# Placing the first expert tiles with float32r products of high and low parts, on one Trainium2 core

## The chip, the cores and the metric

The kernel runs on one core of a Trainium2 chip. The metric is the device time of one execution, in microseconds (us). Engines are named as the profile names them: PE is TensorE, DVE is VectorE, ACT is ScalarE, POOL is GpSimd, SP is the engine that issues most transfers.

## What is computed

The reference is a two layer network on x of 4 x 128 rows of 512 numbers. Each layer is a cross attention, a mixer, and a mixture of eight experts of which every row uses two:

```python
x = x + _L0_xattn_ref(...)   # cross attention on 2048 context rows
x = x + _L0_attn_ref(...)    # retention
x = x + _L0_ffn_ref(_layernorm(x, axis=-1), ...)
x = x + _L1_xattn_ref(...)
x = x + _L1_attn_ref(...)    # a linear recurrence
x = x + _L1_ffn_ref(_layernorm(x, axis=-1), ...)

# L0_ffn: two of 8 experts a row, 512 -> 2048 -> 512
logits = silu(x @ rw1 + rb1) @ rw2 + rb2
k_logits, k_index = top_k(logits, 2)
k_prob = softmax(k_logits)
h = silu(xf @ w1[e] + b1[e]) @ w2[e] + b2[e]     # added with weight we of that row and expert
# L1_ffn: two of 8 experts a row, 512 -> 512 -> 512
router_logits = x_flat @ router_w + router_b
activated = silu(sorted_tokens @ we_gate[e]) * (sorted_tokens @ we_up[e])
ff_out = activated @ we_down[e]
```

## The kernel before, in words

The program is six stages in a row, each with its own streams of instructions on the five engines and a barrier between stages. The change is in one function, `stage_experts`, which is run twice: as the third stage (names `moe0_...`, some 836 to 1290 us in the trace, called the first experts here, `first` is true) and as the sixth (`moe1_...`, 2017 to 2210 us, the second experts).

**Precision.** Products that must be exact to float32 are made in one of two ways. A product of two float32 operands is one instruction in the program and two records in the trace. Or both operands are cut into a float32r high part and the float32r rest (hi and lo), and three products are summed in PSUM (`three_products`, lines 91 to 95). Weights are cut this way: ACT casts the block (`high`, L1835), DVE subtracts (`low`, L2012). `lo_done` says that the low part is there.

**Tiles.** The rows that an expert gets are sorted into tiles of 128 slots, 15 tiles (NT). `g` counts groups of 512 hidden columns: 60 groups in the first experts (4 a tile), 15 in the second. For every group PE does `expand` (12 products with 512 columns, `three_products` over four parts of a tile's rows), `turn_h` (4 transposes) and `contract` (12 products). ACT copies the result of `expand` out of PSUM (`kept`, L1926), applies silu (L1937), and casts the next weights. DVE cuts low parts. The tile's own turned rows have to be cut too: ACT casts the bank XB to `xThi` (`high_x`, L1843), then DVE subtracts that from the bank to `xTlo` (`low_x`, L2104), and `expand` waits for it.

**Start of the stage.** Rows are normalised on DVE (`xn`, L1991), turned by PE, the router's scores are made (L1669, L1688), and a chain of small DVE instructions (L2027 to L2064) works out each row's two slots. Then three things go on together:
- POOL scatters the rows `xn` by slot to DRAM with eight indirect transfers (L1631). SP waits for them (`scattered`) and reads the tiles back (`load_rows`, L1579); all later weight loads stand behind this in SP's queue.
- The first tile does not wait for that. DVE writes a matrix of zeros and ones (`here`, L2071, L2074), and PE multiplies `xn` by it (`place_first`, 16 float32 products with 128 columns, L1702) into XB. In the second experts the second tile is made in the same way (`place_next`, L1711).
- The last two tiles (LATE) are never read back row by row: ACT makes their matrices (`late_distances` L1900, `late_shares` L1908), DVE adds them (`add_late`, L2121), and PE turns them (`turn_late`, L1725).

The order on every engine is the order in which the Python code emits it. In the first experts PE has `place_first`, `turn_late` twice, then the groups; ACT has `late_distances`, `late_shares`, `high_x(0)`; DVE has `add_late`, `low_x(0)`, `low(1, 0)`.

Of the kernel before, what the change touches and what calls it, by code (L numbers as in the profile page):

```python
# [25 lines left out]
P = 128  # L26
D = 512
C = D // P
NB = 4
# [1395 lines left out]
def stage_experts(nc, k, name, t, x, x_out, xg, od, layer, prefetch):  # L1425
# [29 lines left out]

    with ExitStack() as ctx:
# [33 lines left out]
        else:  # L1490
# [5 lines left out]
        here = xT[:, 3, :].rearrange("p (b t) -> p b t", b=NB)  # L1496
        next_1st, next_2nd = rows_in[:, 6, :], rows_in[:, 7, :]
        here_next = xT[:, 1, :].rearrange("p (b t) -> p b t", b=NB)
# [24 lines left out]
                                    "we", "we_turned", "weT", "y_made", "y_added", "b1_more", "out", "stored", "summed", "squared", "low_slots", "apart", "near", "next", "late_apart", "low_prob", "late_near")}  # L1523
# [17 lines left out]
        with nc.Block() as block:  # L1541
# [71 lines left out]
            def _(pool):  # L1613
# [14 lines left out]
                nc.gpsimd.tensor_copy(rw2_wide[:, :, 0:NE], rw2[:]).then_inc(s_["wide"], 1)  # L1628
                pool.wait_ge(s_["slots"], 1)
# [12 lines left out]
            def _(pe):  # L1642
# [54 lines left out]

                def place_first():
                    for b in range(NB):
                        pe.wait_ge(s_["here"], b + 1)  # L1700
                        for c in range(C):
                            last = pe.matmul(XB[:, c * P:(c + 1) * P], xn[:, b, c * P:(c + 1) * P], here[:, b, :],  # L1702
                                             start=(b == 0 and c == 0), stop=(b == NB - 1), skip_group_check=True)
                    last.then_inc(x_turned, 1)

                def place_next():
                    pe.wait_ge(xlo_done, 1)
                    pe.wait_ge(s_["next"], 1)
                    for b in range(NB):
                        for c in range(C):  # L1710
                            last = pe.matmul(XB[:, c * P:(c + 1) * P], xn[:, b, c * P:(c + 1) * P], here_next[:, b, :],  # L1711
                                             start=(b == 0 and c == 0), stop=(b == NB - 1), skip_group_check=True)
# [40 lines left out]
                def expand(bank, kind, g):  # L1753
                    i = g // GR
                    pe.wait_ge(lo_done[kind], g + 1)
                    pe.wait_ge(xlo_done, i + 1)
# [764 lines left out]
```

## Time and profile before

| | us |
|---|---|
| median of three runs | 2216.48 |
| lowest and highest | 2208.49, 2216.7 |
| the profiled execution | 2211.86 |
| its span | 2209.9 |
| PE busy in the span | 2097.7 (95%) |
| DVE, ACT, POOL busy | 1395.0, 1390.7, 297.0 |

The profiled execution is one of its own beside the three runs; every duration below is from it. Its span is 2.0 us shorter than its time, which is what lies around the span. In the page's 40 slices the second experts lie in the last three and a half.

### The profile page before, as it was taken

How to read it: one execution, taken by the hardware profiler on the slowest of the kernel's cores; microseconds unless marked ns; L12 is line 12 of the kernel's file. 1: busy time of each engine (PE TensorE's matmuls, PEld its weight loads, DVE VectorE, ACT ScalarE, POOL GpSimd, SP SyncE). 2: the span in 40 equal slices, each digit the busy share in tenths (PEclk: the TensorE clock that was granted, in tenths of full speed). 3: DMA queues.
4: the chain of work that ended last, by engine and by line, in shares of the span. 5: the costliest groups of instructions: out<-in, count | busy, mean ns of one | idle time of the engine just before them, and what ended most of it. 6: DMA issues, size and time to landing. Idle time of an engine off the chain costs nothing. (4 is left out here: it accounts for less than half of the span.)

```text
span 2209.9 us, 37941 instructions
## 1 busy us (share of the span) xinstructions
PE 2097.7 (95%) x14773; PEld 1629.5 (74%) x14773; DVE 1395.0 (63%) x2384; ACT 1390.7 (63%) x2685; POOL 297.0 (13%) x268
## 2 busy tenths in 40 slices
PE   7999999999999989799999989999999999977998
PEld 4788788777775556688888857887877777755775
DVE  6555455455555753699999965445454555577887
ACT  4666566566655444788888845665665666555774
POOL 1212112112100000100000201211111121102001
PEclk9999999999999989999999999999999999998999
DMA  4001000010104002799999830001010010013996
GB/s 162 20 20 40 20 23 37 20 39 20 39 20 149 26 13 99 294 383 381 351 364 363 334 110 20 20 20 39 20 39 20 20 40 20 20 58 115 367 358 236
DMA packets 53792, 262.04 MB, mean 119 GB/s; under 512 B 9576, under 2 KB 9960, under 8 KB 26992
## 3 DMA queue, kind: packets, MB, share of 16 engines
q1 hardware_dynamic: 47312, 244.42, 29.7%
q0 software_dynamic: 2560, 8.39, 1.1%
q10 hardware_dynamic: 3744, 6.82, 0.8%
q8 instruction: 119, 1.95, 0.4%
q14 instruction: 57, 0.47, 0.1%
HBM read 243.61 MB, written 15.99 MB: 117 GB/s over the span
## 5 line engine op out<-in xcount | busy, mean ns | idle before, releaser
L611 DVE COPY c_pt<-bank 128x512 f32<-128x512 f32 x256 | 177.1, 692 | 556.3 <-PE bank L426 556.3
L808 ACT ACTIVATE c_pr<-wide,c_nmax 128x512 f32<-128x512 f32 x512 | 348.9, 697 | 138.7 <-DVE c_nmax L603 71.6
L295 POOL TENSOR_TENSOR c_clo<-land,c_chi 128x512 fp32r<-128x512 f32 x120 | 154.4, 1288 | 992.6 <-ACT c_chi L777 992.6
L426 PE MATMUL bank<-ident,c_pr 128*128 128x128 f32 x2048 | 268.2, 274 | 3.4 <-DVE c_pt L611 2.7
L426 PEld LDWEIGHTS bank<-ident,c_pr 128*128 128x128 f32 x2048 | 239.8, 141 | 37.7 <-DVE c_pt L611 3.6
L791 ACT ACTIVATE c_khi<-bank,c_cols 128x512 fp32r<-128x512 f32 x128 | 88.0, 688 | 252.1 <-PE bank L95 252.1
L93 PE MATMUL bank<-c_wv_hi,c_chi 128*128 128x512 f32 x512 | 218.4, 427 | 18.4 <-DVE c_clo L542 17.1
L93 PE MATMUL bank<-c_chi,c_wk_hi 128*128 128x512 f32 x512 | 214.1, 418 | 0.3 <-DVE c_wk_lo L534 0.2
L94 PE MATMUL bank<-c_wv_lo,c_chi 128*128 128x512 f32 x512 | 203.2, 397 | 0.0
L95 PE MATMUL bank<-c_wv_hi,c_clo 128*128 128x512 f32 x512 | 202.9, 396 | 0.0
L95 PE MATMUL bank<-c_chi,c_wk_lo 128*128 128x512 f32 x512 | 202.5, 395 | 0.0
L94 PE MATMUL bank<-c_clo,c_wk_hi 128*128 128x512 f32 x512 | 199.4, 389 | 0.0
L815 ACT COPY c_pt<-bank 128x512 f32<-128x512 f32 x256 | 150.3, 587 | 63.1 <-PE bank L426 63.0
L603 DVE CUSTOM_DVE_ANT_0 wide<-wide,land 128x512 f32<-128x512 f32 x256 | 169.2, 724 | 3.7 <-PE wide L410 3.3
L606 DVE TENSOR_REDUCE c_nmax<-wide 128x1 f32<-128x512 f32 x256 | 158.9, 684 | 3.4 <-PE wide L410 3.1
L2012 DVE TENSOR_TENSOR moe_wlo<-moe_hr,moe_whi 128x2048 fp32r<-128x2048 f32 x68 | 153.3, 2285 | 5.1 <-ACT moe_whi L1835 5.1
L93 PE MATMUL wide<-moe_whi,moe_xThi 128*128 128x512 f32 x360 | 143.9, 400 | 10.2 <-DVE moe_xTlo L2104 8.4
L93 PEld LDWEIGHTS bank<-c_wv_hi,c_chi 128*128 128x128 f32 x512 | 97.1, 190 | 62.1 <-issue 24.2
L95 PE MATMUL wide<-moe_whi,moe_xTlo 128*128 128x512 f32 x360 | 141.8, 394 | 0.0
L94 PE MATMUL wide<-moe_wlo,moe_xThi 128*128 128x512 f32 x360 | 141.8, 394 | 0.0
L442 PEld LDWEIGHTS bank<-c_pt,c_v 128*32 128x32 f32 x4096 | 104.1, 110 | 48.9 <-issue 46.9
L442 PE MATMUL bank<-c_pt,c_v 128*32 128x128 f32 x4096 | 138.3, 276 | 1.6 <-ACT c_pt L815 1.6
(428 smaller groups left out, 4248.6 us busy)
## 6 DMA issues: line engine op xcount, KB each, us to landing
moe_hr<-in_L_ffn_w SPq DMA_DIRECT2D x68, 1024.0 KB, 7.0
land<-in_L_ffn_w SPq DMA_DIRECT2D x34, 1024.0 KB, 7.6
land<-in_ctx SPq DMA_DIRECT2D x31, 1024.0 KB, 4.9
moe_raw<-in_L_ffn_w SPq DMA_DIRECT2D x18, 1024.0 KB, 7.2
moe_raw<-in_L_ffn_we_gate SPq DMA_DIRECT2D x8, 1024.0 KB, 7.2
land<-in_L_ffn_we_up SPq DMA_DIRECT2D x8, 1024.0 KB, 6.9
moe_raw<-in_L_ffn_we_down SPq DMA_DIRECT2D x8, 1024.0 KB, 8.1
moe_raw<-in_L_ffn_we_up SPq DMA_DIRECT2D x7, 1024.0 KB, 7.7
```

The lines of the kernel that those rows point to most:

```text
L93: pe.matmul(out, w_hi, m_hi, start=start, stop=False, skip_group_check=not check)
L94: pe.matmul(out, w_hi, m_lo, start=False, stop=False, skip_group_check=not check)
L95: return pe.matmul(out, w_lo, m_hi, start=False, stop=stop, skip_group_check=not check)
L295: nc.gpsimd.tensor_tensor(clo[:, g % 2, c, :], raw[:, c, :], f32(chi[:, g % 2, c, :]), ALU.subtract) \
L426: last = pe.transpose(TB[n % 2][:, h * P:(h + 1) * P], pr[:, u % 2, h, n * P:(n + 1) * P], k["ident"][:])
L442: last = pe.matmul(OB[h * HD:(h + 1) * HD, 0:P], v[:, (T4 * g + n) % VR, at:at + HD], pt[:, n, h * P:(h + 1) * P], start=(n == 0), stop=(n ...
L603: nc.vector.tensor_tensor_reduce(S[h][:], S[h][:], hidden[:, i * CH:(i + 1) * CH], -1.0, BIG, ALU.add, ALU.min, into).then_inc(max_done, 1)
L606: nc.vector.tensor_reduce(into, S[h][:], AX.X, ALU.max, negate=True).then_inc(max_done, 1)
L611: nc.vector.tensor_copy(pt[:, n, :], TB[0][:]).then_inc(pt_dve, 1)
L808: nc.scalar.activation(pr[:, u % 2, h, :], S[h][:], ACT.Exp, bias=nmax[:, b % 2, i, at:at + 1], scale=-1.0 if masked else 1.0, accum_out=d ...
L815: nc.scalar.copy(pt[:, n, :], TB[1][:]).then_inc(pt_act, 1)
L2012: nc.vector.tensor_tensor(wlo[kind][:, g % 2, :], raw[n % RW], f32(whi[kind][:, g % 2, :]), ALU.subtract).then_inc(lo_done[kind], 1)
```

## The change

`here`, `here_next` and the rows that are placed become float32r. ACT casts `xn` to `xn_hi` (`high_rows`, four casts of 128x512), POOL subtracts to `xn_lo` (four subtractions of 128x512). `place` multiplies the high parts into XB and the low parts into a second bank, XLO: 32 products where there were 16. Since a matrix of zeros and ones only picks rows, XB then holds the high parts and XLO the low ones, and `low_x` of these tiles is a copy of XLO that waits for PE alone, not for `high_x`. In the second experts ACT takes two of the four copies of the turned rows. In the first experts `high_x(0)` goes ahead of `late_shares`, `low_x(0)` ahead of `add_late`, and `turn_late` behind the first `expand`.

```diff
-        here = xT[:, 3, :].rearrange("p (b t) -> p b t", b=NB)
+        here = hlo[:, 0, :].rearrange("p (b t) -> p b t", b=NB)
+        xn_hi, xn_lo = (tile[KINDS - 1][:, 1, :].rearrange("p (b d) -> p b d", b=NB) for tile in (whi, wlo))
+        XLO = (ps_of[4], ps_of[5])
...
+                if first:
+                    pool.wait_ge(s_["h_made"], HT)
+                for b in range(NB):
+                    pool.wait_ge(s_["xn_hi"], b + 1)
+                    nc.gpsimd.tensor_tensor(xn_lo[:, b, :], xn[:, b, :], f32(xn_hi[:, b, :]), ALU.subtract).then_inc(s_["xn_lo"], 1)
                 pool.wait_ge(s_["slots"], 1)
...
-                        if not first:
+                        if not first and q < 2:
                             pe.wait_ge(s_["xT"], q + 1)
+                        elif not first:
+                            pe.wait_ge(s_["xT_late"], q - 1)
...
+                def place(i, taker, b):
+                    for to, rows in ((XB, xn_hi), (XLO[i], xn_lo)):
+                        for c in range(C):
+                            last = pe.matmul(to[:, c * P:(c + 1) * P], rows[:, b, c * P:(c + 1) * P], taker[:, b, :],
+                                             start=(b == 0 and c == 0), stop=(b == NB - 1), skip_group_check=True)
+                    return last
...
                 place_first()
                 if first:
-                    for l in range(LATE):
-                        turn_late(l)
                     for g in range(NG + 2):
                         if g < NG:
                             after(pe, kept, g - 1)
                             expand(HB[g % 2], 0, g).then_inc(hid_made, 1)
+                        if g == 0:
+                            for l in range(LATE):
+                                turn_late(l)
...
+                def high_rows():
+                    for b in range(NB):
+                        act.wait_ge(s_["xn"], b + 1)
+                        nc.scalar.copy(xn_hi[:, b, :], xn[:, b, :]).then_inc(s_["xn_hi"], 1)
...
+                    high_rows()
                     high(1, 0)
                 else:
+                    high_rows()
+                    for c in (2, 3):
+                        act.wait_ge(s_["turned"], c + 1)
+                        nc.scalar.copy(xT[:, c, :], ps[c][:]).then_inc(s_["xT_late"], 1)
                     high(0, 0)
...
                 if first:
                     late_distances()
+                    high_x(0)
                     late_shares()
-                    high_x(0)
...
                 def low_x(i):
-                    dve.wait_ge(xhi_done, i + 1)
-                    last = nc.vector.tensor_tensor(xTlo[:, i % 2, :], XB[:], f32(xThi[:, i % 2, :]), ALU.subtract)
+                    if i < (1 if first else 2):
+                        dve.wait_ge(x_turned, i + 1)
+                        last = nc.vector.tensor_copy(xTlo[:, i % 2, :], XLO[i][:])
+                    else:
+                        dve.wait_ge(xhi_done, i + 1)
+                        last = nc.vector.tensor_tensor(xTlo[:, i % 2, :], XB[:], f32(xThi[:, i % 2, :]), ALU.subtract)
...
                 if first:
                     weigh_pairs()
+                    low_x(0)
                     add_late()
-                    low_x(0)
                     low(1, 0)
```

How instructions stand on the engines. ACT in the first experts, from the last Silu of the router to the first copy of a hidden group; `moe_e` is the Exp of the router, `moe_in_late` `late_distances`, `moe_prob` `late_shares`, `moe_xThi` `high_x(0)`, the last row `kept(0)`. Before:

```order
L1874 ACTIVATE moe_hr<-bank,moe_rb 128x512 x8
L1835 CAST moe_whi<-land 128x2048
L1885 ACT_TABLE_LOAD
L1885 ACTIVATE moe_e<-moe_gap 128x4
L1900 ACTIVATE moe_big<-moe_in_late,moe_low_slot 128x2x128 x8
L1908 ACTIVATE moe_big<-moe_big,moe_prob,moe_low_prob 128x2x128 x8
L1843 CAST moe_xThi<-bank 128x512
L1926 COPY moe_xT<-wide 128x512
```

The same place now:

```order
L1896 ACTIVATE moe_hr<-bank,moe_rb 128x512 x8
L1877 CAST moe_whi<-moe_xn 128x512 x4
L1851 CAST moe_whi<-land 128x2048
L1912 ACT_TABLE_LOAD
L1912 ACTIVATE moe_e<-moe_gap 128x4
L1927 ACTIVATE moe_big<-moe_in_late,moe_low_slot 128x2x128 x8
L1859 CAST moe_xThi<-bank 128x512
L1935 ACTIVATE moe_big<-moe_big,moe_prob,moe_low_prob 128x2x128 x8
L1953 COPY moe_xT<-wide 128x512
```

Four casts of rows stand ahead of a weight cast, and `high_x(0)` stands ahead of `late_shares`.

DVE in the first experts, after the slots: `moe_back_i` ends `weigh_pairs`, `moe_big` is `add_late`, `moe_xTlo` is `low_x(0)`, then `low(1, 0)` and `low(0, 2)`. Before:

```order
L2093 CAST moe_back_i<-moe_back_f 128x8
L2121 TENSOR_TENSOR moe_big<-moe_big 128x512 x2
L2104 TENSOR_TENSOR moe_xTlo<-bank,moe_xThi 128x512
L2012 TENSOR_TENSOR moe_wlo<-land,moe_whi 128x2048
L2012 TENSOR_TENSOR moe_wlo<-moe_hr,moe_whi 128x2048
```

The same place now:

```order
L2120 CAST moe_back_i<-moe_back_f 128x8
L2132 CAST moe_xTlo<-bank 128x512
L2152 TENSOR_TENSOR moe_big<-moe_big 128x512 x2
L2039 TENSOR_TENSOR moe_wlo<-land,moe_whi 128x2048
L2039 TENSOR_TENSOR moe_wlo<-moe_hr,moe_whi 128x2048
```

The subtraction has become a cast out of the second bank and has moved ahead of `add_late`.

POOL in the first experts, where the rows' low parts are cut. Before:

```order
L1628 COPY moe_ob<-moe_rw 128x16x8
L1631 DMA slot_rows<-moe_xn,moe_slot_i 1920x512 x8
```

The same place now:

```order
L1631 COPY moe_ob<-moe_rw 128x16x8
L1636 TENSOR_TENSOR moe_wlo<-moe_xn,moe_whi 128x512 x4
L1639 DMA slot_rows<-moe_xn,moe_slot_i 1920x512 x8
```

Four subtractions stand between the router's copy and the eight scatters.

## Rows read from the trace of the kernel before

**Rows 1.** The page's first part: busy time of the engines over the whole span.

```profile
PE 2097.7 (95%) x14773; PEld 1629.5 (74%) x14773; DVE 1395.0 (63%) x2384; ACT 1390.7 (63%) x2685; POOL 297.0 (13%) x268
```

**Rows 2.** Busy time by stretch: PE, PEld, DVE, ACT, POOL, clock, DMA share, GB/s.

```profile
915.00:1275.00 360.00, 356.11 (x1706) 293.73 (x1704) 340.24 (x269) 314.81 (x432) 15.21 (x8) 1.00 0.94 361
2052.00:2176.00 124.00, 118.61 (x554) 97.14 (x555) 106.78 (x74) 96.23 (x91) 0.00 (x0) 0.97 0.98 370
```

**Rows 3.** Who waited for whom, 915 to 1275 us, then from 2052 us.

```profile
PE bank L93 <- DVE moe_hlo L2149: 1.4, 1, 1.4
...
ACT moe_whi L1835 <- DMA land<-in_L_ffn_we_down: 7.2, 6, 1.8
```

**Rows 4.** Timeline, first experts: start, length, engine, line, operation [idle before <-releaser].

```profile
900.14 5.74 PE L1702 MATMUL bank<-moe_xT,moe_xn 128*128 128x128 f32 x32 [3.21 <-DVE moe_xT L2074]
902.89 4.04 ACT L1908 ACTIVATE moe_big<-moe_big,moe_prob,moe_low_prob 128x256 f32<-128x256 f32 x8 [0.23 <-DVE moe_low_prob L2123]
906.83 0.56 ACT L1843 CAST moe_xThi<-bank 128x512 fp32r<-128x512 f32 x1
906.96 1.29 DVE L2121 TENSOR_TENSOR moe_big<-moe_big 128x512 f32<-128x512 f32 x2 [3.09 <-ACT moe_big L1908]
...
909.00 0.47 PE L93 MATMUL wide<-moe_whi,moe_xThi 128*128 128x512 f32 x1
...
911.84 0.39 PE L93 MATMUL wide<-moe_whi,moe_xThi 128*128 128x512 f32 x1
...
914.77 0.58 ACT L1926 COPY moe_xT<-wide 128x512 f32<-128x512 f32 x1 [0.28 <-PE wide L95]
...
925.51 0.67 ACT L1843 CAST moe_xThi<-bank 128x512 fp32r<-128x512 f32 x1
```

**Rows 5.** Timeline, second experts.

```profile
2021.61 2.48 DVE L2007 COPY moe_xT<-wide 128x512 f32<-128x512 f32 x4 [1.61 <-PE wide L1646]
...
2033.77 5.55 PE L1702 MATMUL bank<-moe_xT,moe_xn 128*128 128x128 f32 x32 [3.29 <-DVE moe_xT L2074]
...
2036.69 3.29 ACT L1900 ACTIVATE moe_big<-moe_in_late,moe_low_slot 128x256 f32<-128x256 f32 x8
...
2039.88 0.56 ACT L1843 CAST moe_xThi<-bank 128x512 fp32r<-128x512 f32 x1
...
2040.48 0.69 DVE L2104 TENSOR_TENSOR moe_xTlo<-bank,moe_xThi 128x512 fp32r<-128x512 f32 x1 [1.39 <-ACT moe_xThi L1843]
...
2049.50 0.38 SPq L1579 DMA_DIRECT2D moe_big<-slot_rows  x1
...
2050.61 0.58 ACT L1843 CAST moe_xThi<-bank 128x512 fp32r<-128x512 f32 x1 [2.52 <-PE bank L1711]
...
2055.35 0.33 SPq L1554 DMA_DIRECT2D land<-in_L_ffn_we_down  x1
```

**Rows 6.** Timeline: weight loads of float32 products with 8 and with 128 columns.

```profile
892.15 0.97 PEld L1688 LDWEIGHTS bank<-moe_fold,moe_ob 128*128 128x128 f32 x8 [1.85 <-issue]
...
2046.62 3.77 PEld L1711 LDWEIGHTS bank<-moe_xT,moe_xn 128*128 128x128 f32 x32
```

**Rows 7.** Timeline, cross attention: a DVE addition with and without POOL at work.

```profile
664.72 0.62 POOL L341 TENSOR_TENSOR c_part<-c_part,c_wn 128x256 f32<-128x256 f32 x1
664.87 0.62 DVE L634 TENSOR_TENSOR c_acc<-c_acc,c_part 128x128 f32<-128x128 f32 x1 [0.49 <-POOL c_acc L338]
...
1947.56 0.29 DVE L634 TENSOR_TENSOR c_acc<-c_acc,c_part 128x128 f32<-128x128 f32 x1
```

**Rows 8.** Groups and instructions that price the rows' high and low parts.

```profile
L295 POOL TENSOR_TENSOR c_clo<-land,c_chi 128x512 fp32r<-128x512 f32 x120 | 154.4, 1288 | 992.6 <-ACT c_chi L777 992.6
...
L2327 ACT CAST rwkv_hi<-rwkv_rise x4: 621/622/624, 1997.9 to 2005.8; 128x512 fp32r<-128x512 f32 x4
...
889.39 0.69 ACT L1874 ACTIVATE moe_hr<-bank,moe_rb 128x512 f32<-128x512 f32 x1 [2.03 <-PE bank L95]
...
894.78 0.23 DVE L2039 TENSOR_TENSOR moe_chosen<-moe_number,moe_bidf 128x64 f32<-128x64 f32 x1
```

More of the change, by code:

```diff
@@ L1454, in stage_experts @@
     place = {block: n for n, block in enumerate(stream)}
+    ps_of = k["ps"]
     with ExitStack() as ctx:
@@ L1522, in stage_experts @@
                                     "logits_kept", "logits", "gap", "e2", "filled", "cut", "taken", "seen", "ranked", "slots", "owners", "scattered",
-                                    "we", "we_turned", "weT", "y_made", "y_added", "b1_more", "out", "stored", "summed", "squared", "low_slots", "apart", "near", "next", "late_apart", "low_prob", "late_near")}
+                                    "we", "we_turned", "weT", "y_made", "y_added", "b1_more", "out", "stored", "summed", "squared", "low_slots", "apart", "near", "next", "late_apart", "low_prob", "late_near", "xn_hi", "xn_lo", "xT_late")}
         xg_in = [m.sem(f"xg{i}") for i in range(4)]
@@ L1700, in place_first @@
                         pe.wait_ge(s_["here"], b + 1)
-                        for c in range(C):
-                            last = pe.matmul(XB[:, c * P:(c + 1) * P], xn[:, b, c * P:(c + 1) * P], here[:, b, :],
-                                             start=(b == 0 and c == 0), stop=(b == NB - 1), skip_group_check=True)
+                        pe.wait_ge(s_["xn_lo"], b + 1)
+                        last = place(0, here, b)
                     last.then_inc(x_turned, 1)
                 def place_next():
-                    pe.wait_ge(xlo_done, 1)
+                    pe.wait_ge(xhi_done, 1)
                     pe.wait_ge(s_["next"], 1)
                     for b in range(NB):
-                        for c in range(C):
-                            last = pe.matmul(XB[:, c * P:(c + 1) * P], xn[:, b, c * P:(c + 1) * P], here_next[:, b, :],
-                                             start=(b == 0 and c == 0), stop=(b == NB - 1), skip_group_check=True)
+                        last = place(1, here_next, b)
                     last.then_inc(x_turned, 1)
@@ L1755, in expand @@
                     pe.wait_ge(lo_done[kind], g + 1)
+                    pe.wait_ge(xhi_done, i + 1)
                     pe.wait_ge(xlo_done, i + 1)
@@ L2004, in _ @@
                         nc.vector.tensor_tensor(xT_lo(c), ps[c][:], f32(xT_hi(c)), ALU.subtract).then_inc(s_["xT"], 1)
-                    else:
+                    elif c < 2:
                         dve.wait_ge(s_["turned"], c + 1)
@@ L2073, in _ @@
                     for b in two:
-                        nc.vector.scalar_tensor_tensor(out=here[:, b, :], in0=in_tile[:], scalar=slot_f[:, b, 1:2], in1=here[:, b, :],
+                        nc.vector.scalar_tensor_tensor(out=here[:, b, :], in0=in_tile[:], scalar=slot_f[:, b, 1:2], in1=f32(here[:, b, :]),
                                                        op0=ALU.is_equal, op1=ALU.add).then_inc(s_["here"], 1)
@@ L2131, in _ @@
                     dve.wait_ge(s_["near"], 2)
-                    nc.vector.tensor_tensor(xT[:, 1, :], next_1st, next_2nd, ALU.add).then_inc(s_["next"], 1)
+                    nc.vector.tensor_tensor(hlo[:, 1, :], next_1st, next_2nd, ALU.add).then_inc(s_["next"], 1)
                     low_x(0)
```

2 lines of the change are left out of this document (1 added, 1 removed).

## The prediction

> **What bounds the kernel now.** I read the page first: PE is busy 95% of the span [rows 1], but the change touches only two starts of stages, so the whole says little. Next come the stretches of the two expert stages. Behind the start of the first experts PE is busy 356.1 of 360 us at the full clock and no engine is far from full (DVE 340, ACT 315) [rows 2]: this stretch has no slack, so whatever its start loses or gains arrives at the end one for one. Behind the start of the second experts the DMA engines are busy 0.98 of the time [rows 2] and ACT waits for weights to land [rows 3]: there the end follows the stream of loads, and an earlier start counts only as far as it makes the loads earlier. Then I read the timelines of the two starts, where the sum is made.
>
> **First experts, the slots.** ACT gets four casts of 0.62 us [rows 8] behind the router's last Silu, which ends at 890.08 [rows 8]. They push `high(1,0)` and the Exp's table by 2.5 us. Nothing waits for these for over 5 us; their cover is ACT's wait for the slots, and without it they would cost those 2.5 us. POOL gets four subtractions of 1.29 us [rows 8], from about 890.75: the third would run to 894.6, the fourth to 895.9 or a little later. POOL itself is idle there, the scatters wait for slots at 899. But DVE is then in the chain of small instructions that makes the slots, and a DVE instruction with two inputs in SBUF does not run beside POOL's: an addition that takes 0.29 us alone took 0.62 us and ended 0.15 us behind the POOL instruction that had started before it [rows 7]. The comparison at 894.78 [rows 8] has two such inputs; it would stand until the fourth subtraction ends, 896.1 if the subtraction of gaps just ahead of it slips in between the third and the fourth. That is +1.3 us for slots, scatters and `place_first`. Bounds: 0 (no conflict) and 1.6 (one more stop, at the third). The nearest row is the one with the conflict, so I take 1.3. The Trainium skill says this in SBUF — State Buffer, section "SBUF: two separate sides": the port pair that VectorE and GpSimd share is an exclusive lock for the whole instruction, and a VectorE instruction with two SBUF inputs takes part in it. It speaks against this change; the trace agrees with its 0.62 for 0.29 us, and without it this term would be 0.
>
> **PE's placing.** 16 float32 products, 32 records, become 32 float32r products. Does a record get shorter with one pass? Eight loads with only 8 moving columns behind each came every (0.97 - 0.19) / 7 = 0.111 us; the 32 with 128 columns every (3.77 - 0.19) / 31 = 0.115 us [rows 6]. Sixteen times the columns cost 0.004 us: it is the load of 128x128 weights that sets the pace, and there are 32 loads before and after. So I take placing as unchanged, 5.74 us in the first experts (most of it at the lower clock) [rows 4] and 3.77 us for `place_next`. No row has a float32r product with 128 columns. Bounds a record: below, half, if the weights no longer set the pace; above, what one with 512 columns takes, (911.84 - 909.00) / 12 = 0.237 us [rows 4]. Both are rivals below.
>
> **First experts, the new order.** `late_shares` (4.04 us) ran beside placing and ended at 906.93 [rows 4]. Now it stands behind `high_x(0)`, which waits for placing. Without POOL's 1.3: placing ends at 905.88, `high_x(0)` and the copy of XLO are over at 906.6, and the first `expand` starts near 906.7 instead of 909.00. That is the gain, 2.3 us. But PE then has `turn_late`: `late_shares` ends at 906.5 + 4.04 = 910.5, `add_late` (1.29 for two) at 911.9, the second turn at about 912.5, and the second `expand` starts at 912.5 where it started at 911.84 [rows 4]: +0.7. Which of the two counts? The second `expand` releases the ACT copy at 914.77, and from there ACT is busy without a gap through silu, weight casts and the late tiles' copies to the cast of the next tile at 925.51 [rows 4], for whose sequel PE waits 1.4 us [rows 3]. So what the second `expand` loses goes to the end, and the first one's 2.3 us are spent in PE's wait for `turn_late`. DVE's `low(1,0)` and `low(0,2)` also stand behind `add_late` now: they end at 911.9 + 2 x 2.3 = 916.5, near the 916.8 of before, so without POOL's term they release the third `expand` no later. SP's reload behind `low(1,0)` is about 3 us later, but no ACT cast waited for a load in this stage. First experts: +0.7 + 1.3 = +2.0 us.
>
> **Second experts.** Four DVE copies in a row took 2.48 us [rows 5]. With ACT taking two, the last is ready after the third turn plus 2 x 0.62, near 2023.3 instead of 2024.09: -0.8 for scores, slots and all that follows, scatters included. POOL's subtractions fall where DVE reads PSUM and end before the slots: 0. `late_distances` held ACT until 2039.98 and so `high_x(0)` [rows 5], 0.7 us later than placing, 2033.77 + 5.55 = 2039.3; both move by -0.8, and `expand` no longer waits for the 0.69 us subtraction behind the 0.56 us cast [rows 5]: `expand(0)` -1.4. `place_next`, the cast at 2050.61 and, through ACT's weight cast and DVE's low part, the load at 2055.35 could move by -1.4 [rows 5]; the stream itself starts when the scatters have landed, 2049.50, and moves by -0.8. With the DMA engines full from there I take -1.0 (bounds -0.5 and -1.4). The second saving of 0.7 behind `place_next` goes into the wait for loads.
>
> **The sum.** +2.0 - 1.0 = +1.0 us. Against the profiled execution, 2211.86 us, that is 2212.9. The median of the three runs is 4.6 us above that execution, which gives 2217.5. I name the middle, **2215 us**: no change that can be told. A measurement of this kernel tells about 0.5%, 11 us, from none.
>
> **Rivals.**
> - *Narrow float32r products are slow* (ends slower). Each of the 32 takes as long as one with 512 columns, 0.237 us at the full clock [rows 4], twice the 0.115 assumed. For: no row excludes it, and full rate was only ever seen here with 512 columns. Against: 128 columns are a quarter of the streaming. Place: the two placings and `place_next`. With some 4 us at the lower clock in front, which then do 9 records instead of 19, each `place_first` is about 3.7 us longer and `place_next` 3.6. First experts +3.7. In the second, `place_first`, which ended 0.7 us ahead of `late_distances` [rows 5], would outlast it by 3 us, and with `place_next` the load at 2055.35 comes some 5 us late instead of 1.4 early: about +5.5 against the sum. It decides from the point where a record exceeds about 0.13 us. Total +1.0 + 9.2 = +10.2: 2222.1 on the profiled scale, 2226.7 on the median's.
> - *They are fast.* At half the 0.115 us: placing 2.4 us shorter in the first experts, all of it on the path (-2.4), `place_next` -1.9, of which the loads let through perhaps 0.5. Total -1.9: 2210. Against: [rows 6]. The Trainium skill has such a rule (TensorE: Matmul & The Clock Gate, "Back-to-back issue gap"): an isolated product takes its columns over the clock plus a small constant, 56 ns with 128 columns. By it, `place_next` would take 32 x 0.056 = 1.8 us; the rows with 8 columns contradict it for products that each load weights.
> - *POOL and DVE do not collide*, because the four casts come late or DVE slips through. The 1.3 goes: -0.3 in all, 2211.6. For: only instructions with two SBUF inputs are hit, and few are in that stretch.
> - *The change does not do what it says*: the reordering is there, but the 0.7 lost in the first experts and the 1.3 are taken up by gaps that I take for ACT's chain, and the loads do not follow the second experts' earlier start. Then the time is that of before, 2211.9. Against: the chain from 914.77 to 925.51 has no gap [rows 4].
>
> **How the numbers follow.** Forecast 0.40, slow narrow products 0.22, fast ones 0.15, no collision 0.15, no effect 0.05, others 0.03. The runs of before spread over 8 us, so every case is smeared by about 4 us to either side. The low end is the fast case, 2210, less 3: 2207. The high end is the slow case on the median's scale: 2226. Outside lie some 2 in 10. Slower by over 0.5% needs the slow case and a run on the high side, 0.22 x 0.4, and 0.01 from the rest: 0.10. Faster by over 0.5% no mechanism gives; the spread alone leaves 0.04. Within: 0.86.
>
> **What would show it.** Right: 32 placing records of about 0.115 us each in `place_next`; `high_x(0)` and the XLO copy side by side; in the first experts a PE gap of some 3 us between the first and second `expand`, filled only by `turn_late`, with the second `expand` about 2 us later against the stage's start; the comparison of the chosen experts stretched from 0.23 to over 1 us beside a POOL subtraction; the second experts about 1 us shorter. Wrong: a pace in `place_next` above 0.13 or below 0.09 us; no DVE instruction stretched; a second `expand` no later than before; or a time off by more than the spread, which would have to come from the clock or the loads in stretches whose instructions the change leaves alone.

## The result, and the profile after

| | before | after |
|---|---|---|
| device time, median | 2210.32 us (20 runs, 2205.53 to 2218.65) | 2215.04 us (20 runs, 2210.31 to 2220.62) |
| ratio | | 1.0021 [1.0012, 1.0030] |
| profiled execution, span | 2209.9 us | 2212.6 us |
| granted TensorE clock, mean over the executions timed | 0.981 | 0.976 |

The changed kernel is slower by 0.21%, some 4.6 us. The three runs shown of before had been high: their median was 2216.48, that of 20 runs is 2210.32. So the time of 2215.04 agrees with the number forecast, 2215, by luck: the sum behind it was +1.0 us, a fifth of what the change costs, and the rest came from a median of before that stood too high.

The last row of the table says where to look. A mean clock of 0.981 over 2210 us is (1 - 0.981) x 2 x 2210 = 84 us at the lower of the two levels (1.2 GHz, 0.50 in the rows); the 0.976 of after, 0.9757 before rounding, is 108 us. Busy time by stretch, in the columns of [rows 2], first of the kernel before, over the two starts of the expert stages:

```profile
894.00:904.00 10.00, 5.42 (x24) 5.29 (x25) 7.96 (x49) 4.62 (x12) 3.54 (x4) 0.50 1.01 423
904.00:909.00 5.00, 3.15 (x25) 2.57 (x24) 2.04 (x4) 3.39 (x7) 3.78 (x5) 0.98 0.58 222
2031.00:2037.00 6.00, 3.23 (x15) 3.23 (x16) 5.48 (x27) 4.00 (x11) 3.02 (x3) 0.50 0.23 87
2040.00:2052.00 12.00, 10.14 (x64) 8.98 (x64) 8.52 (x11) 9.45 (x14) 5.05 (x4) 1.00 0.59 215
```

and of the kernel after:

```profile
893.00:912.00 19.00, 13.47 (x49) 12.13 (x50) 9.82 (x45) 8.29 (x19) 8.72 (x9) 0.50 0.70 287
912.00:929.00 17.00, 14.44 (x74) 11.67 (x72) 11.59 (x10) 15.13 (x20) 0.00 (x0) 0.99 0.98 381
930.00:932.00 2.00, 2.00 (x6) 1.52 (x6) 2.00 (x2) 2.00 (x5) 0.00 (x0) 0.50 0.98 414
915.00:1275.00 360.00, 356.12 (x1706) 294.58 (x1705) 337.87 (x266) 315.54 (x433) 15.36 (x8) 1.00 0.94 358
2029.50:2049.00 19.50, 14.77 (x53) 13.14 (x54) 13.89 (x45) 15.16 (x33) 10.69 (x8) 0.50 0.60 214
2052.00:2176.00 124.00, 118.20 (x573) 95.56 (x573) 106.78 (x76) 95.77 (x88) 0.00 (x0) 1.00 0.95 364
```

Before, the clock fell when PE ran out of work behind the router and rose again inside the placing, at about 904 and 2037. After, it stayed at 0.50 until 912 and 2049, through all of the placing and the whole first `expand`, and it fell once more at about 930. The long stretches behind the starts (915 to 1275, 2052 to 2176) look as in [rows 2], except that the second had the clock at 0.97 before and at 1.00 in this execution. Timeline of the first experts after, to hold against [rows 4]:

```profile
887.99 2.16 ACT L1877 CAST moe_whi<-moe_xn 128x512 fp32r<-128x512 f32 x4
888.75 4.95 POOL L1636 TENSOR_TENSOR moe_wlo<-moe_xn,moe_whi 128x512 fp32r<-128x512 f32 x4 [48.21 <-ACT moe_whi L1877]
892.46 1.27 DVE L2061 TENSOR_TENSOR moe_gap<-moe_best 128x4 f32<-128x4 f32 x1
893.85 0.23 DVE L2066 TENSOR_TENSOR moe_chosen<-moe_number,moe_bidf 128x64 f32<-128x64 f32 x1
...
899.22 1.12 PE L1711 MATMUL bank<-moe_hlo,moe_whi 128*128 128x128 f32 x4 [3.21 <-DVE moe_hlo L2101]
...
905.25 1.05 PE L1711 MATMUL bank<-moe_hlo,moe_wlo 128*128 128x128 f32 x4
906.35 0.59 ACT L1859 CAST moe_xThi<-bank 128x512 fp32r<-128x512 f32 x1 [4.62 <-PE bank L1711]
906.35 0.69 DVE L2132 CAST moe_xTlo<-bank 128x512 fp32r<-128x512 f32 x1 [3.41 <-PE bank L1711]
906.83 4.04 ACT L1935 ACTIVATE moe_big<-moe_big,moe_prob,moe_low_prob 128x256 f32<-128x256 f32 x8
907.18 0.77 PE L93 MATMUL wide<-moe_whi,moe_xThi 128*128 128x512 f32 x1 [0.88 <-issue]
907.75 0.63 PE L94 MATMUL wide<-moe_wlo,moe_xThi 128*128 128x512 f32 x1
...
912.40 1.04 PE L1739 MATMUL bank<-ident,moe_big 128*128 128x128 f32 x8
913.20 0.48 PE L93 MATMUL wide<-moe_whi,moe_xThi 128*128 128x512 f32 x1
...
929.58 0.77 PE L93 MATMUL bank<-moe_whi,moe_hhi 128*128 128x512 f32 x1 [2.30 <-DVE moe_hlo L2180]
930.15 0.63 PE L94 MATMUL bank<-moe_wlo,moe_hhi 128*128 128x512 f32 x1
```

Placing takes 906.30 - 899.22 = 7.08 us instead of 5.74, one product every 0.213 us. The first `expand` takes 5.2 us instead of 2.8 (12 products every 0.43 instead of 0.237 us). DVE's subtraction of the gaps stands 1.27 instead of 0.15 us: it ends at 893.73, with POOL's fourth subtraction (893.70). Second experts after, to hold against [rows 5]:

```profile
2034.91 1.12 PE L1711 MATMUL bank<-moe_hlo,moe_whi 128*128 128x128 f32 x4 [3.29 <-DVE moe_hlo L2101]
...
2040.94 1.05 PE L1711 MATMUL bank<-moe_hlo,moe_wlo 128*128 128x128 f32 x4
2042.04 0.59 ACT L1859 CAST moe_xThi<-bank 128x512 fp32r<-128x512 f32 x1 [0.93 <-PE bank L1711]
...
2042.88 0.77 PE L93 MATMUL wide<-moe_whi,moe_xThi 128*128 128x512 f32 x1 [0.88 <-DVE moe_xTlo L2132]
...
2049.72 0.38 SPq L1582 DMA_DIRECT2D moe_big<-slot_rows  x1
...
2051.28 0.56 PE L1711 MATMUL bank<-moe_hlo,moe_whi 128*128 128x128 f32 x4
...
2054.36 0.61 PE L1711 MATMUL bank<-moe_hlo,moe_wlo 128*128 128x128 f32 x4
2055.01 0.59 ACT L1859 CAST moe_xThi<-bank 128x512 fp32r<-128x512 f32 x1 [4.24 <-PE bank L1711]
```

`place_next`, at the full clock, takes 3.69 us for 32 products, one every 0.112 us: the pace that the forecast read from [rows 6]. The 7.1 us of the placing is the same work at half the clock.

**A ledger for all kernels.** Stages start at other times in each execution, so points are counted from a landmark. First experts: from the start of DVE's copy of the router's parts (`moe_ob<-bank`, 891.34 in the kernel before, 889.36 after). Second experts: from the stage's square root (`moe_std`, 2017.36 and 2019.04). "Contraction" is the one behind PE's wait for `moe_hlo` ([rows 3]; 928.11 - 891.34 = 36.77 before, 929.58 - 889.36 = 40.22 after), "join" the first product with `moe_b` at the stage's end (1273.19 and 1276.18), "second cast" the second `high_x` of the second experts (2050.61 and 2055.01). Each place is from one execution; clock and time are from all executions of a kernel, the time as a ratio to the kernel before in the same batch, where the mean clock of before was 0.981 or 0.982.

| kernel | first `expand` | contraction | join | second cast | clock | time, % [95%] |
|---|---|---|---|---|---|---|
| before | 17.66 | 36.77 | 381.85 | 33.25 | 0.981 | 0 |
| e1_order | 15.45 | 36.70 | 381.76 | 33.28 | 0.982 | -0.03 [-0.15, 0.08] |
| e5_split | 17.65 | 36.74 | 381.80 | 32.97 | 0.981 | +0.05 [-0.07, 0.17] |
| e2_products | 19.05 | 40.02 | 384.53 | 34.59 | 0.976 | +0.36 [0.24, 0.47] |
| e4_nosub | 16.34 | 39.10 | 385.24 | 36.10 | 0.975 | +0.32 [0.21, 0.43] |
| after | 17.82 | 40.22 | 386.82 | 35.97 | 0.976 | +0.21 [0.12, 0.30] |
| e7_float32 | 21.78 | 43.64 | 389.71 | 34.95 | 0.978 | +0.55 [0.41, 0.70] |
| e3_warm | 15.53 | 37.41 | 382.41 | 32.94 | 0.982 | +0.19 [0.08, 0.30] |
| e6_before_warm | 17.43 | 37.51 | 382.01 | 34.59 | 0.983 | +0.15 [0.05, 0.26] |
| e8_b_all | 14.37 | 35.62 | 382.30 | 34.17 | 0.984 | +0.14 [0.04, 0.24] |
| e10_first_only | 17.81 | 40.16 | 386.67 | 32.79 | 0.978 | +0.25 [0.15, 0.35] |
| e11_second_only | 15.96 | 37.21 | 382.29 | 36.29 | 0.979 | +0.08 [-0.02, 0.19] |
| e12_after_swap | 17.82 | no wait | 383.35 | 35.96 | 0.976 | +0.17 [0.08, 0.26] |
| e9_swap | 15.98 | no wait | 380.34 | 33.00 | 0.981 | -0.07 [-0.17, 0.04] |
| e13_after_bridge | 14.94 | no wait | 379.97 | 31.37 | 0.985 | -0.03 [-0.12, 0.06] |
| e14_before_bridge | 14.36 | no wait | 378.89 | 34.16 | 0.984 | -0.06 [-0.18, 0.05] |

From contraction to join it is 345.1 us before and 346.6 after; in every kernel with that wait 344.5 to 346.7. The larger ones are those whose clock fell at the contraction. After it PE has one more wait, of 0.7 us just ahead of the join, before and after alike.

### The profile page after: what moved, and what is told of

Same layout as the page of the kernel before. It is cut to its first block and busy times, and to the rows that moved or that the text cites. A ratio compares the mean times of both kernels' runs of the same rounds, so it can differ in the third digit from the quotient of the medians.

```text
span 2212.6 us, 38052 instructions
## 1 busy us (share of the span) xinstructions
PE 2102.4 (95%) x14773; PEld 1632.4 (74%) x14773; DVE 1395.0 (63%) x2382; ACT 1397.7 (63%) x2695; POOL 304.6 (14%) x276
```

## Experiments

### Which part of the change costs

**e1_order**: the kernel before, with only the new order (late shares behind `high_x(0)`, late tiles added behind `low_x(0)` and turned behind the first `expand`).

```diff
                 if first:
                     late_distances()
-                    late_shares()
                     high_x(0)
+                    late_shares()
...
-                    add_late()
                     low_x(0)
+                    add_late()
...
```

> The kernel before with the new order of the first experts alone: the cast of the first tile ahead of the late shares, the late tiles turned behind the first expand; float32 products as before. Theory (the kind of product decides the clock): the clock rises to 2.4 GHz inside placing as before, placing takes 5.5 to 5.8 us in both stages, and the second expand starts 0.7 us later than before against the router's end; time +0.3 to +1.0 us against before. Rival (order or chance decides the clock): placing takes about 6.8 us at 1.2 GHz in at least one stage, and the kernel is 2 us or more slower.

Measured: -0.03% [-0.15, 0.08]. PE's timeline:

```profile
908.53 0.47 PE L93 MATMUL wide<-moe_whi,moe_xThi 128*128 128x512 f32 x1 [1.49 <-DVE moe_xTlo L2105]
912.39 1.26 PE L1725 MATMUL bank<-ident,moe_big 128*128 128x128 f32 x8 [0.89 <-DVE moe_big L2122]
...
929.78 0.47 PE L93 MATMUL bank<-moe_whi,moe_hhi 128*128 128x512 f32 x1 [2.55 <-DVE moe_hlo L2150]
```

The first `expand` starts 2.2 us earlier, and the contraction when it did: PE's wait for `moe_hlo` grew from 1.41 to 2.55 us and the rest went into the late turn, now between two expansions. The order neither gains nor costs.

**e2_products**: the changed kernel with the order of before.

```diff
...
+                    late_shares()
                     high_x(0)
-                    late_shares()
...
```

> The changed kernel with the order of before in the first experts: float32r products, POOL subtractions, ACT copies stay. Theory: both placings take 6.8 us wholly at 1.2 GHz, and the first expand behind them starts there too; one subtraction on DVE is stretched to over 1 us; time +2 to +4.5 us against before. Rival (the order is the cost): placing back at 5.7 us or below, time within 1 us of before.

Measured: +0.36% [0.24, 0.47], mean clock 0.976, placing 7.1 us, contraction at 40.02. All of the loss is there without the new order. In us it is 8 (5 to 10 by the interval), more than the 2 to 4.5 expected and than the changed kernel's 4.6; no trace explains the excess, and the two intervals overlap.

**e5_split**: the kernel before with two of the four copies of the second experts' turned rows on ACT.

```diff
+                    for c in (2, 3):
+                        act.wait_ge(s_["turned"], c + 1)
+                        nc.scalar.copy(xT[:, c, :], ps[c][:]).then_inc(s_["xT_late"], 1)
...
-                    else:
+                    elif c < 2:
                         dve.wait_ge(s_["turned"], c + 1)
                         nc.vector.tensor_copy(xT[:, c, :], ps[c][:]).then_inc(s_["xT"], 1)
```

> The kernel before with only the copies of the second experts' turned rows split between VectorE and ScalarE. By my sum -0.8 us; slots of the second experts 0.5 us earlier behind the square root (14.7 instead of 15.3). Rival: the three other engines hide it and it is within 0.05% of before. The clock's low stretches as in the kernel before, mean granted clock of its executions 0.981.

Measured: +0.05% [-0.07, 0.17]. The second cast comes 0.28 us earlier (32.97 for 33.25), and nothing of it can be told in the time (-0.8 us had been expected).

**e4_nosub**: the changed kernel without POOL's subtractions. It leaves out the low parts of the rows: the same 32 products read a low tile that no subtraction wrote (in the second experts one of zeros).

```diff
-                    nc.gpsimd.tensor_tensor(xn_lo[:, b, :], xn[:, b, :], f32(xn_hi[:, b, :]), ALU.subtract).then_inc(s_["xn_lo"], 1)
...
-                        pe.wait_ge(s_["xn_lo"], b + 1)
+                        pe.wait_ge(s_["xn_hi"], b + 1)
```

> The changed kernel without POOL's four subtractions: the placed rows have no proper low part (the second product reads what stands in that tile), nothing else is left out. Theory of the shared port: the subtraction of the gaps on DVE takes 0.15 instead of 1.27 us, slots and placing come 1.1 us earlier against the router's end, and the kernel is 1.1 us faster than the changed one. Rival: the 1.27 us has another cause and stays, or goes without any gain in time.

Measured: +0.32% [0.21, 0.43], no better than the changed kernel. The subtraction of the gaps is back at 0.15 us and the slots come 1.5 us earlier, but clock and placing (7.1 us) stay, the contraction moves by only 1.1 us, and its wait grows to 2.62. So POOL's subtractions do hold DVE up, and that isn't the loss.

### Whether it is the clock

**e3_warm**: the changed kernel with 8 and 12 unread products of 512 columns in PE's waits ahead of the placing.

```diff
+                def keep_busy(n):
+                    pe.wait_ge(hi_done[0], 1)
+                    for _ in range(n):
+                        pe.matmul(ps[0][:], whi[0][:, 0, 0:P], whi[0][:, 0, 0:D], start=True, stop=True)
...
+                keep_busy(12)
                 place_first()
```

> The changed kernel with products that nobody reads in two waits of PE ahead of placing (8 behind the router's logits, 12 ahead of placing, 512 columns each, into the bank that expand overwrites). Theory (the clock is what makes it slower): PE is at 2.4 GHz when placing starts, the 32 products take 3.7 instead of 6.8 us, the first expand 2.8 instead of 5.4, and the kernel gets 3 to 6 us faster than the changed one, about as fast as before or 1 us faster. Rival (POOL's lock and the order are the cost, the clock falls off the path): placing gets shorter, but the time stays within 1 us of the changed kernel.

**e6_before_warm**: the same lines in the kernel before.

> The kernel before with 8 and 12 unread 512-column products ahead of placing, in time in which TensorE waits. Theory A (the low clock's place sets the time): placing runs at the full level from its start in both experts' stages, 3.8 us instead of 5.7 and 5.6, and high_x comes some 1.5 us earlier in each: 2207 to 2208 against 2210. Theory B (the unread products cost something by themselves, which is why the changed kernel with them was still 0.19% slower than before): 2212 to 2214 although placing is as quick as in A. If the first experts' later part (fourth kept hidden tile to the first joining product) has its length of before, and the time is still longer, the loss lies outside the stages that the products touch.

**e8_b_all**: the kernel before with these lines, the new order and the split copies.

> The kernel before with the change's order, its two copies on ScalarE in the second experts, and the unread products, but with the placing products of before (one set, full float32) and no rounding or subtraction for them. Theory A: what the parts gained singly adds up: order 0 to -1, copies -0.6 (slots were 0.5 us earlier in the changed kernel's second experts), clock -3: 2206 to 2207 against 2210. Theory B: the unread products cost what they gain: 2210 to 2213.

Measured, in this order: +0.19% [0.08, 0.30], +0.15% [0.05, 0.26], +0.14% [0.04, 0.24]. The placing runs at the full clock in all three (3.8 us), yet none gains. Stretches of e3_warm:

```profile
890.00:907.00 17.00, 11.96 (x79) 9.30 (x76) 11.04 (x57) 9.71 (x18) 10.49 (x10) 1.00 0.79 312
907.50:910.50 3.00, 3.00 (x9) 2.32 (x8) 0.09 (x1) 2.88 (x6) 2.01 (x3) 0.50 0.48 183
911.00:930.00 19.00, 15.84 (x80) 12.72 (x79) 14.01 (x12) 17.13 (x26) 0.00 (x0) 1.00 0.94 366
```

and PE's waits in e6_before_warm, with the low clock behind them:

```profile
907.38 1.83 PE L1731 MATMUL bank<-ident,moe_big 128*128 128x128 f32 x8 [3.72 <-issue]
908.86 0.78 PE L93 MATMUL wide<-moe_whi,moe_xThi 128*128 128x512 f32 x1
...
2041.41 0.77 PE L93 MATMUL wide<-moe_whi,moe_xThi 128*128 128x512 f32 x1 [3.70 <-DVE moe_xTlo L2111]
```

In the first experts of e3_warm and e6_before_warm the quick placing only lengthens PE's wait behind it (2.3 and 3.7 us), the clock falls in that wait, and part of the first `expand` runs at 0.50. In e8_b_all the clock holds there and falls at the contraction, behind a wait of 2.55 us; in the second experts it falls in the first expansions of all three. I had expected the placing alone to decide; that was wrong. From their ledger rows e3_warm should have been level with before, and it is 4 us over. That left a rival: unread products might cost some 3 us by themselves.

**e7_float32**: the changed kernel with the first placing's products read as plain float32, two records each.

```diff
+                    read = f32 if i == 0 else (lambda a: a)
...
-                            last = pe.matmul(to[:, c * P:(c + 1) * P], rows[:, b, c * P:(c + 1) * P], taker[:, b, :],
+                            last = pe.matmul(to[:, c * P:(c + 1) * P], read(rows[:, b, c * P:(c + 1) * P]), read(taker[:, b, :]),
```

> The changed kernel with the 32 products of the first placing read as plain float32, so that each leaves two records: 64 instead of 32. Theory A1 (the one-pass kind of the products is what left the clock low): the clock rises inside placing as in the kernel before, after some 24 records, the rest run at 0.115 us: placing 9.5 to 10 us instead of 7.1, but the first expand is back at 2.75 us instead of 5.4, so that the kept hidden tiles come when they come in the changed kernel; mean granted clock of the executions back at 0.981 from 0.976; time 2215 to 2216. Theory A2 (narrow products with a weight load each leave it low, whatever the kind, and in the kernel before the rise came by something else): all 64 at 0.213 us, 13.6 us, and the time 6 to 12 us over the changed kernel.

```profile
899.96 2.07 PE L1712 MATMUL bank<-moe_hlo,moe_whi 128*128 128x128 f32 x8 [3.21 <-DVE moe_hlo L2102]
...
905.24 1.50 PE L1712 MATMUL bank<-moe_hlo,moe_wlo 128*128 128x128 f32 x8
906.57 1.06 PE L1712 MATMUL bank<-moe_hlo,moe_whi 128*128 128x128 f32 x8
```

```profile
893.00:905.00 12.00, 6.61 (x29) 6.48 (x30) 8.77 (x47) 4.50 (x10) 5.87 (x7) 0.50 0.90 373
906.00:930.00 24.00, 20.36 (x116) 16.98 (x116) 12.01 (x9) 16.38 (x27) 2.89 (x3) 1.00 0.74 285
```

Six microseconds out of each first placing, of the changed kernel and of this one, show how busy PE was:

```profile
899.50:905.50 6.00, 6.00 (x30) 6.00 (x30) 3.13 (x17) 2.23 (x6) 4.47 (x6) 0.50 0.67 266
```

```profile
900.00:906.00 6.00, 6.00 (x28) 6.00 (x29) 3.36 (x18) 2.46 (x7) 4.48 (x5) 0.50 0.73 294
```

The records come at the same 0.213 us as the one-pass products, from the same tiles into the same banks, but the clock rises inside, at about 906, some 6 us after the placing's start (3.5 us in the second experts); the one-pass products had 7.1 us and the expansion behind them and did not raise it before 912. So the kind of product matters (theory A1). The placing takes 10.3 us, a little over the 9.5 to 10 expected (9.1 us in the second experts). The time does not come out: +0.55% [0.41, 0.70] from five runs, where 2215 to 2216 (+0.25%) was expected. The quicker expansion does not make up for the placing: the contraction is 3.4 us later than in the changed kernel.

### Which stage

**e10_first_only** and **e11_second_only**: the changed kernel with the new products in one stage, and those of before in the other.

```diff
-                    for to, rows in ((XB, xn_hi), (XLO[i], xn_lo)):
+                    for to, rows in ((XB, xn_hi), (XLO[i], xn_lo)) if new else ((XB, xn),):
```

> The changed kernel with the placing products of before in the second experts (order and split copies stay): the new products in the first experts alone. Clock theory: placing 7.1 us at the low level, first expand 5.4 us, the contraction behind the last wait at 40.2 instead of 36.7; second experts as before less 0.3: +3 to +4 us over before, mean granted clock of its executions 0.978 to 0.979. Rival (the loss sits in the second experts, where every us of TensorE is on the path): +1 or less.

> The changed kernel with the placing products of before in the first experts: the new products in the second experts alone. Clock theory: first experts as with the order alone (contraction at 36.7), second experts' second high_x at 36.0 instead of 33.3 (two first expands at the low clock): +1.5 to +2.5 us over before, mean granted clock 0.978 to 0.979; the excesses of this kernel and of the one with the first experts alone add up to the changed kernel's 4.6. Rival: the other way round, +4 here and +1 there.

Measured: +0.25% [0.15, 0.35] and +0.08% [-0.02, 0.19], clocks 0.978 and 0.979. The first experts carry the larger part of the loss. With the new products in the second experts alone the second cast is 3.0 us later (36.29); the interval of the time, nothing to 4 us, doesn't tell whether that reaches the end. The two add up to 0.33, against 0.21 with intervals of 0.1 on each.

### The last wait of the first experts

**e12_after_swap**: the changed kernel with DVE splitting the hidden tile before it subtracts the next row tile's high part; the split had stood behind a wait of 2.1 us for ACT.

```diff
-                        if g % GR == 2 and g // GR + 1 < NT:
-                            low_x(g // GR + 1)
                         if 1 <= g <= NG:
...
                                 .then_inc(hlo_done, 1)
+                        if g % GR == 2 and g // GR + 1 < NT:
+                            low_x(g // GR + 1)
```

> The changed kernel with VectorE's split of the hidden tile ahead of the next row tile's subtraction. Theory A: the wait of 2.30 us in front of the contraction goes, and with it the second fall of the clock that came behind it (8 products at 0.43 instead of 0.23, 1.6 us): contraction at 38 instead of 40.2, first joining product at 383 instead of 386.8, time 2211.5 to 2212.5 instead of 2215. Theory B (load stream): 2214 to 2215.

**e9_swap**: the kernel before with the new order, the split copies and this swap.

> The kernel before with the change's order, its split of the copies, and one more edit: VectorE splits the hidden tile (moe_hhi, moe_hlo) before it subtracts the next row tile's high part, for which it waits on ScalarE. Theory A (the last wait of TensorE in the first experts, in front of the contraction some 37 us behind the product of the router's parts, sets their end, 345 us later): the order alone brought the first expand 2.2 us forward and lost it in that wait, which grew from 1.41 to 2.55 us; with the wait gone the contraction starts some 2.3 us earlier (34.4 instead of 36.7), the clock doesn't fall behind it, and the time is 2207 to 2208 against 2209.5. Theory B (the load stream is what limits there, at a DMA share of 0.97): TensorE waits later instead and the time stays within 0.05% of before.

Timelines of e12_after_swap and of e9_swap; the contraction's first product has no wait in front of it:

```profile
926.71 0.69 DVE L2178 TENSOR_TENSOR moe_hlo<-moe_xT,moe_hhi 128x512 fp32r<-128x512 f32 x1
927.73 0.48 PE L93 MATMUL bank<-moe_whi,moe_hhi 128*128 128x512 f32 x1
```

```profile
923.25 0.69 DVE L2153 TENSOR_TENSOR moe_hlo<-moe_xT,moe_hhi 128x512 fp32r<-128x512 f32 x1
924.09 0.47 PE L93 MATMUL bank<-moe_whi,moe_hhi 128*128 128x512 f32 x1
```

In the trace the places came as foretold: join at 383.35 (expected 383) and at 380.34, contraction at 927.73 - 890.10 = 37.6 and 924.09 - 889.63 = 34.5. The times moved less. e12 is at +0.17% [0.08, 0.26], its 2211.96 us inside the range expected, but against a before that ran 1.4 us lower in this batch than beside the changed kernel; e9 is at -0.07% [-0.17, 0.04]. Neither gain can be told from nothing by the time alone.

### The clock held up all the way

**e13_after_bridge**: e12_after_swap with the unread products of e3_warm, and 8 more behind the first placing.

```diff
+                keep_busy(12)
                 place_first()
+                keep_busy(8)
```

> The changed kernel with VectorE's swap, 8 and 12 unread products ahead of placing, and 8 more behind the first placing, in the wait for high_x and its low part. Theory A (the clock alone: with unread products ahead only, it fell again in TensorE's wait of 2.3 and 3.0 us behind the placing, and the first expand ran at the low level for 3.4 us, which took back part of the gain): no low stretch from the placing to the third expand in either stage, first expand 2.75 us, contraction (or the wait in its place) some 4.5 us earlier than in the changed kernel, second high_x of the second experts at 31.5 instead of 36.0, and 2208 to 2209.5, level with before. Theory B (unread products cost 3 us or more by themselves, whatever the clock): 2211 or more, although the profiled stretches are as A says.

**e14_before_bridge**: e9_swap with the same lines.

> The kernel before with the order, the split copies, VectorE's swap (this was 0.07% under before) and the same unread products, 8, 12 and 8. Theory A: another 1.5 to 2 us less in the second experts (second high_x at 31.5 instead of 33.0) and up to 1.5 in the first: 2205 to 2207 against 2209. Theory B: 2210 to 2212, the 3 us of the unread products on top of 2208.2.

Measured, in this order: -0.03% [-0.12, 0.06] and -0.06% [-0.18, 0.05]. Stretches of e13_after_bridge, and PE between placing and first `expand`:

```profile
888.00:930.00 42.00, 36.21 (x201) 28.69 (x194) 29.24 (x72) 32.99 (x52) 13.00 (x12) 1.00 0.82 329
2025.00:2060.00 35.00, 32.05 (x180) 26.83 (x180) 28.45 (x64) 28.54 (x42) 10.12 (x8) 1.00 0.76 282
```

```profile
902.06 0.61 PE L1717 MATMUL bank<-moe_hlo,moe_wlo 128*128 128x128 f32 x4
902.51 2.06 PE L1704 MATMUL wide<-moe_whi 128*128 128x512 f32 x8
904.40 0.40 PE L93 MATMUL wide<-moe_whi,moe_xThi 128*128 128x512 f32 x1
```

e13 differs from e12 in nothing but unread products, which add work to PE, and it is faster: +0.17% [0.08, 0.26] became -0.03% [-0.12, 0.06], level with before. Two pairs say it more closely. e12 and e9 differ only in what the new placing brings (its products, ACT's casts, POOL's subtractions), and so do e13 and e14; each pair was timed in one batch. Without unread products the median of e12 is 3.7 us above that of e9 (2211.96 and 2208.24); with them e13 is 0.7 us below e14 (2208.05 and 2208.71). So where the clock is held up the new placing costs nothing that these runs can tell: the loss of the changed kernel is the low clock that comes with it. It also tells against the rival: 28 unread products a stage do not cost 3 us whatever the clock. In the kernel before they gain nothing (e14 against e9: -0.06% and -0.07%). There the clock fell once more in the second experts' first `expand`, the second cast came at 34.16 where 31.5 was expected, and 2205 to 2207 was missed at 2208.7. No kernel here beats the one before by more than its interval.

**What stays open.** The two shifts of a ledger row (join, second cast) give the time only within some 4 us: e13's add up to -3.8 us and its time is -0.7, e3_warm's to +0.3 and +4, e2_products' to +4.0 and +8, the changed kernel's to +7.7 and +4.6. A row is one execution, and the executions of one kernel lie up to 13 us apart. Nor does the mean clock alone give the time: that of e3_warm, 0.982, is that of before, and its time is 4 us over. Whether unread products cost 1 to 3 us elsewhere when the clock falls again behind them (e3, e6, e8) was not settled.

## Why the prediction was wrong

- **"So I take placing as unchanged, 5.74 us"** is the step that failed. The pace per product was right: 0.115 forecast, 0.112 measured at the full clock, 0.213 at the lower. But 5.74 us was already a sum over both levels: before, the clock rose inside this very placing. I carried the time over without asking what had raised the clock. With the new products it did not rise: placing 7.1 us (+1.3), first `expand` 5.2 us (+2.4), and in the second experts both expansions of the first group from 2042.88 to 2051.28, 8.4 us where they had taken 5.5. The second `expand` of the first experts, forecast 2.0 us later, came 3.3 us later (913.20 - 889.36 = 23.84 for 20.50), and the join 5.0 us later. No term of the sum let the clock change, and the rival of slow products took its 4 us at the lower clock over from before in the same way; "would have to come from the clock" stood only in the last sentence, for stretches that the change leaves alone.
- **POOL's lock, +1.3 us**: nearly the right size, on another instruction. The subtractions began where forecast, 0.6 us ahead of the landmark, but followed one another every 1.23 us and not every 1.29. So the fourth began just ahead of the gap subtraction, which was to have slipped in before it, and that one was stretched (+1.12 us, slots at 8.79 instead of 7.74) rather than the comparison of the chosen experts (0.23, untouched). For the time it hardly counts (e4_nosub).
- **The new order, +0.7 us**: e1_order gave -0.2 at the second `expand` (20.32 for 20.50 behind the landmark) and -0.1 at the contraction. The shape was right, a gain of 2.2 us (2.3 forecast) at the first `expand` that is lost in the waits for the late turn and `moe_hlo`; the 0.7 was too much.
- **"This stretch has no slack"**: right. Contraction to join is 344.5 to 346.7 us in all kernels, and 3.45 us at the contraction were 4.97 at the join. What was missed is the 1.5 between: behind the longer wait, 2.30 us, the clock was low again.
- **Second experts, -1.0 us**: the copies gained 0.3 to 0.5 instead of 0.8 (slots at 14.72 instead of 15.26 in the changed kernel, 14.94 in e5_split). The second cast moved by +2.7 instead of -1.4. Of that little reached the time (e11_second_only, +0.08%, not told from none).
- **The rivals**: narrow products were neither slow (0.112 us) nor fast at the full clock. The slow case had the right place and sign, products at nearly twice the price (0.213 us); but the price came from the clock, so it applied to `place_first` and the first expansions and not to `place_next`.
- **The scale**: I added half of the 4.6 us by which the three runs' median stood over the profiled execution. On 20 runs that median was 6 us lower. That is why the number looks right and the sign was missed. Within 0.5%, given 0.86, held.

## What to carry to other kernels

A duration that spans a change of the clock is not a property of the instructions. Split it at the rise, price both parts, and ask which work raised the clock and whether the change keeps that work; if it is replaced by a cheaper kind, price everything up to the next likely rise at the lower level. Where a stretch behind a last wait runs without gaps, the time hangs on when that wait ends: an earlier start ahead of it only makes the wait longer, and a longer wait can lower the clock.

## What the runs showed of the hardware

- 32 one-pass (float32r) products with 128 columns, back to back for 7.1 us, left the granted clock at 0.50, in all ten placings of this kind that began at that level: in e2_products, e4_nosub, e10_first_only, e11_second_only, e12_after_swap and the changed kernel. Plain float32 products at the same 0.213 us a record, from the same tiles, had it rise inside (e7_float32), as they did in the kernel before. The Trainium skill (TensorE: Matmul & The Clock Gate, section "The HAM clock gate") says that the clock follows how busy the array was. These two placings were busy alike by the profile, 6.00 of 6.00 us, and differed in the kind of product alone; the measurement says that this matters too, and why stays open.
- A wait of PE of 2.3 to 3.7 us behind a stretch at the full clock was followed by a fall to 0.50 in e3_warm, e6_before_warm and the changed kernel. It is not certain: behind waits of 2.54 to 2.57 us in front of the contraction there was none in e1_order, e3_warm and e11_second_only, and one in e7_float32 and e8_b_all.
- The same kernel's executions differ by some 10 us, and mostly with their mean granted clock (0.979 and 0.983 in e5_split went with 2212.9 and 2205.6 us). Fitted within each kernel over all 284 executions that list a clock, a clock higher by 0.001 goes with 1.5 us less. The clock of many executions told more of the cause than any one trace.
- DVE's subtraction of 128x4 values, 0.15 us alone, took 1.27 us beside POOL's of 128x512 and ended with it.
